# Values of the last two chunks one slot earlier, first keys in four banks, tokens' places one slot later

## The reference

```python
x = x + cross(layernorm(x), ctx)      # 16 heads of 32, stablemax, projections with biases
x = x + self_attention(layernorm(x))  # 8 query heads, one key/value head of 64, causal
x = x + ffn(layernorm(x))             # mean of 2 shared experts + top 2 of 8, hidden 2048
...
shared = (gelu(xf @ sW1 + sb1) @ sW2 + sb2).mean(over the 2 shared)
gates = xf @ rW + rb
topk_vals, topk_idx = top_k(gates, 2)
moe = sum over the chosen e of softmax(topk_vals) * (gelu(xf @ W1[e] + b1[e]) @ W2[e] + b2[e])
return shared + moe
```

## Time and profile before

| | |
|---|---|
| median of 3 runs | 1439.92 us (1439.58 to 1440.78) |
| the profiled execution | 1441.54 us |
| its span, first to last instruction | 1439.8 us |
| TensorE busy | 1390.5 us, 97% |
| VectorE, ScalarE, GpSimd busy | 63%, 56%, 29% |
| TensorE in the chain that ended last | 87% |
| mean granted TensorE clock | 0.987 |

### The profile page before, as it was taken

How to read it: one execution, slowest core, us unless ns; L and a number is a source line. 1 busy time by engine, 2 the same in 40 slices (tenths; PEclk the granted TensorE clock), 3 DMA queues, 4 the chain that set the end, 5 groups by cost and what they waited for, 6 DMA issues and landing times.

```text
span 1439.8 us, 23358 instructions
## 1 busy us (share of the span) xinstructions
PE 1390.5 (97%) x9164; PEld 1252.5 (87%) x9164; DVE 913.5 (63%) x1542; ACT 809.9 (56%) x1453; POOL 414.8 (29%) x219
## 2 busy tenths in 40 slices
PE   6999999999999999999999999879999999999998
PEld 4799999989889889889999989768788999999987
DVE  6456766766776775776675676475566554655665
ACT  3566666655756755756765656454553444545443
POOL 2144353443444434434434434220003000001000
PEclk9999999999999999999999999989999999999999
DMA  5121111011111111011101101084445649999991
GB/s 196 45 92 30 31 34 30 30 63 59 30 70 30 30 63 51 24 60 41 30 30 63 45 30 63 10 347 176 147 154 157 216 162 366 337 354 340 351 397 58
DMA packets 34710, 174.40 MB, mean 121 GB/s; under 512 B 6138, under 2 KB 8346, under 8 KB 18212
## 3 DMA queue, kind: packets, MB, share of 16 engines
q1 hardware_dynamic: 32852, 168.10, 32.6%
q0 software_dynamic: 1744, 4.76, 1.1%
HBM read 166.78 MB, written 6.06 MB: 120 GB/s over the span
## 4 chain that ended last, share of the span: by engine, by line
PE 87%; DVE 6%; ACT 4%; issue 1%; DMA 1%; POOL 0%; PEldq 0%; DVEq 0%; SPq 0%; PEld 0%; POOLq 0%; ACTq 0%
PE bank L680 18%; PE bank L668 17%; PE bank L990 10%; PE bank L700 10%; PE bank L1007 8%; PE po L713 6%; PE bank L852 6%; PE po L869 6%; PE bank L769 1%; PE bank L733 1%; PE bank L725 1%; PE bank L814 1%; DVE tt L1266 1%; ACT tt L1145 1%; DVE sa L1274 1%
## 5 line engine op out<-in xcount | busy, mean ns | idle before, releaser
L552 POOL TENSOR_TENSOR xn<-xn,tt 128x1024 f32<-128x1024 f32 x96 | 237.5, 2474 | 467.4 <-DVE sa L1279 467.4
L1374 DVE TENSOR_TENSOR wsl<-ring,wsh 128x2048 fp32r<-128x2048 f32 x72 | 165.0, 2291 | 118.0 <-ACT wsh L1084 118.0
L668 PE MATMUL bank<-cxh,wkh 128*128 128x256 f32 (+1 forms) x768 | 220.5, 287 | 5.6 <-DVE va L1254 3.2
L668 PE MATMUL bank<-cxl,wkh 128*128 128x256 f32 (+1 forms) x768 | 220.3, 287 | 0.0
L668 PE MATMUL bank<-cxh,wkl 128*128 128x256 f32 (+1 forms) x768 | 220.1, 287 | 0.0
L1247 DVE SCALAR_TENSOR_TENSOR kl<-bank,bkt,kh 128x256 fp32r<-128x256 f32 (+1 forms) x192 | 94.4, 493 | 193.7 <-ACT kh L1042 193.5
L680 PE MATMUL bank<-wvh,cxh 128*128 128x512 f32 (+1 forms) x416 | 165.1, 397 | 2.5 <-DVE kl L1247 2.5
L1140 ACT ACTIVATE tt<-bank 128x512 f32<-128x512 f32 (+1 forms) x208 | 124.1, 599 | 77.0 <-PE bank L700 71.9
L1084 ACT CAST wsh<-ring 128x2048 fp32r<-128x2048 f32 x72 | 137.3, 1907 | 53.2 <-PE po L869 29.6
L680 PE MATMUL bank<-wvl,cxh 128*128 128x512 f32 (+1 forms) x416 | 163.7, 394 | 0.0
L680 PE MATMUL bank<-wvh,cxl 128*128 128x512 f32 (+1 forms) x416 | 163.3, 392 | 0.0
(11 more groups left out here) (237 smaller groups left out, 2954.9 us busy)
## 6 DMA issues: line engine op xcount, KB each, us to landing
ring<-in_w SPq DMA_DIRECT2D x112, 1024.0 KB, 7.0
ctxt<-in_ctx SPq DMA_DIRECT2D x40, 512.0 KB, 3.6
ctxt<-in_ctx SPq DMA_DIRECT2D x8, 642.0 KB, 4.1
wqt<-in_wo SPq DMA_DIRECT2D x4, 1024.0 KB, 5.8
wqt<-in_aq SPq DMA_DIRECT2D x4, 1024.0 KB, 6.4
wqt<-in_ap_ SPq DMA_DIRECT2D x4, 1024.0 KB, 6.4
yrows<-K SPq DMA_DIRECT2D x1, 2048.0 KB, 9.2
tt<-in_wk SPq DMA_DIRECT2D x1, 1024.0 KB, 5.1
```

Of the source, the lines that this page charges most:

```text
L552: e.tensor_tensor(dacc[0:kn, y, :], dacc[0:kn, y, :], tt[0:kn, w, :], ALU.add).then_inc(s["da_pool"], 1)
L668: m = e.matmul(dst[:, 0:n], (wkh, wkl)[a][:, c, g * P:(g + 1) * P], (cxh, cxl)[b][:, u, c, 0:n], start=(c == 0 and x_ == 0), stop=(c == 3 ...
L1374: e.tensor_tensor(wsl[m % 3][:], ring[slot(unit_split(m))][:], wsh[m % 3][:].bitcast(F32), ALU.subtract).then_inc(s["wl_dve"], 1)
```

## The change

Three things. `values_in` gives slot + 2 for every slot up to 101, so chunks 102 and 103 are multiplied in slots 100 and 101. At the start wk is loaded in two halves with part 0 of the context between them, its parts are made in the order of landing, and the keys of part 0 are summed in four banks at once, all groups for each pair of operands (`first_keys`); the warm-up uses `ones`, filled by VectorE, and has 44 matmuls; the values of chunks 0 and 1 move behind the queries on TensorE, ScalarE and VectorE; the turned rows move ahead of the parts of wv; the casts of the patterns and the store of the blank table move back. And `positions` with all that hangs on it moves from `ROUTE` + 1 to `ROUTE` + 2, slot 121 (`PLACE`).

```diff
 ROUTE = NCH + 15
...
 def values_in(slot):
 
-    if slot < NCH - 4:
-        return slot + 2
-    return {NCH - 3: NCH - 2, NCH - 2: NCH - 1}.get(slot)
+    return slot + 2 if slot + 2 < NCH else None
 
...
 
             return 16 * (n // NR + 1)
 
+        def key_bank(i, g):
+            return pj[use["k", i, g] % 2] if i else bank[(0, 1, 4, 5)[g]]
...
                 e.dma_start(ctxt[:, 0:4 * n], ctxs[i % NPT][i // NPT]).then_inc(s["ctx_in"], 16)
 
-            e.dma_start(wkt, wk).then_inc(s["wk_in"], 16)
+            e.dma_start(wkt[:, 0:2, :], wk[:, 0:2, :]).then_inc(s["wk_in"], 16)
             load_ctx(0)
+            e.dma_start(wkt[:, 2:4, :], wk[:, 2:4, :]).then_inc(s["wk2_in"], 16)
             e.dma_start(bkt[:], bk).then_inc(s["bk_in"], 16)
             e.dma_start(xres[:], x).then_inc(s["x_in"], 16)
...
 
-            e.wait_ge(s["zero_dve"], 2)
-            e.dma_start(table.rearrange("(p k) c -> p (k c)", p=P),
...
                 if n == 3:
+                    e.wait_ge(s["zero_dve"], 2)
+                    e.dma_start(table.rearrange("(p k) c -> p (k c)", p=P),
+                                blank[:, :, :].rearrange("p k c -> p (k c)")).then_inc(s["zero_in"], 16)
                     e.wait_ge(s["k2_pool"], 1)
                     e.dma_start(yrows[0:8 * P, :].rearrange("(p a) (b c) -> p (a b) c", p=P, b=2),
...
                             pattern=[[-1, 64]], channel_multiplier=1).then_inc(s["mask_pool"], 1)
             e.wait_ge(s["mask_pool"], 3)
-            e.memset(ones[:], 1.0).then_inc(s["iota_pool"], 1)
+            e.memset(tri[:], 1.0).then_inc(s["iota_pool"], 1)
             e.wait_ge(s["iota_pool"], 1)
...
-            e.wait_ge(s["iota_pool"], 7)
+            e.wait_ge(s["iota_pool"], 6)
             e.memset(qbh[:].bitcast(F32), 0.0).then_inc(s["qz_pool"], 1)
...
                 return pj[u % 2]
+
+            def first_keys():
+
+                n = width(0)
+                for h in range(2):
+                    for x_, (a, b) in enumerate(((0, 0), (1, 0), (0, 1))):
+                        if (h, x_) == (0, 0):
+                            e.wait_ge(s["wkh_act"], 1)
+                            e.wait_ge(s["ch_act"], 1)
+                        elif x_ == 0:
+                            e.wait_ge(s["wkh_act"], 2)
+                        elif x_ == 1:
+                            e.wait_ge(s["wkl_dve"], h + 1)
+                        elif h == 0:
+                            e.wait_ge(s["cl_dve"], 1)
+                        for g in range(4):
+                            for c in (2 * h, 2 * h + 1):
+                                m = e.matmul(key_bank(0, g)[:, 0:n], (wkh, wkl)[a][:, c, g * P:(g + 1) * P],
+                                             (cxh, cxl)[b][:, 0, c, 0:n], start=(x_ == 0 and c == 0),
+                                             stop=(x_ == 2 and c == 3))
+                            if (h, x_) == (1, 2):
...
                     e.wait_ge(s["ch_act"], i + 1)
-                    if i:
-                        e.wait_ge(s["cl_pool"], i)
-                    else:
-                        e.wait_ge(s["wkl_dve"], 2)
-                        e.wait_ge(s["cl_dve"], 1)
+                    e.wait_ge(s["cl_pool"], i)
...
                 m.then_inc(s["pr_pe"], 1)
 
-            e.wait_ge(s["idb_dve"], 1)
-            warm(30, bank[7])
-            for g in range(4):
-                keys(0, g)
-            for n in range(2):
-                values(n)
+            e.wait_ge(s["ones_dve"], 1)
+            warm(44, bank[7])
+            first_keys()
+            e.wait_ge(s["const_pool"], 2)
             for t in range(4):
-                turn(t, bank[2 + t])
+                turn(t, bank[(2, 3, 6, 7)[t]])
             e.wait_ge(s["wq_in"], 16)
...
                 for c in range(4):
                     m = e.matmul(dst[:], wqt[:, c, g * P:(g + 1) * P], xT[:, c, :], start=(c == 0), stop=(c == 3))
                 m.then_inc(s["q_pe"], 1)
+            for n in range(2):
+                values(n)
...
                     shared_up(n - NCH)
-                if n == ROUTE + 1:
+                if n == PLACE:
                     positions()
-                if n == ROUTE + 3:
+                if n == PLACE + 2:
                     turn_weights()
-                if n == ROUTE + 11:
+                if n == PLACE + 10:
                     turn_fetched(0)
                 if n > NCH:
                     shared_down(n - NCH - 1)
-                if n == ROUTE + 5:
+                if n == PLACE + 4:
                     output_biases()
...
                     e.wait_ge(s["s_pe"], 2 * (first(i - 2) + chunks_of(i - 2)))
-                e.activation(kh[:, u, g, 0:n], pj[use["k", i, g] % 2][:, 0:n], ACT.Identity,
+                e.activation(kh[:, u, g, 0:n], key_bank(i, g)[:, 0:n], ACT.Identity,
                              bias=bkt[:, g:g + 1]).then_inc(s["kh_act"], 1)
...
 
             e.preload_act_table_set("natural_log_exp_and_others")
             e.wait_ge(s["wk_in"], 16)
-            for c in (slice(0, 2), slice(2, 4)):
-                e.copy(wkh[:, c, :], wkt[:, c, :]).then_inc(s["wkh_act"], 1)
+            e.copy(wkh[:, 0:2, :], wkt[:, 0:2, :]).then_inc(s["wkh_act"], 1)
             context_hi(0)
+            e.wait_ge(s["wk2_in"], 16)
+            e.copy(wkh[:, 2:4, :], wkt[:, 2:4, :]).then_inc(s["wkh_act"], 1)
             e.wait_ge(s["eps_dve"], 1)
             for t in range(4):
                 root(0, t)
-            keys_hi(0, 0)
-            keys_hi(0, 1)
+            for g in range(4):
+                keys_hi(0, g)
+            turned(0, bank[2])
+            turned(2, bank[6])
             e.wait_ge(s["wv_in"], 16)
             e.copy(wvh[:], wvt[:]).then_inc(s["wvh_act"], 1)
-            keys_hi(0, 2)
-            keys_hi(0, 3)
-            values_hi(0)
-            values_hi(1)
-            turned(0, bank[2])
-            turned(2, bank[4])
             context_hi(1)
...
                              scale=XSCALE).then_inc(s["q_act"], 1)
             for h in range(4):
                 queries_hi(0, h)
+            values_hi(0)
+            values_hi(1)
 
             for n in range(NSLOT):
...
                     e.activation(pr[:, :, 1], pr[:, :, 0], ACT.Exp).then_inc(s["gap_act"], 1)
-                if n == ROUTE + 3:
+                if n == PLACE + 2:
...
                 e.wait_ge(s["kh_act"], 4 * i + g + 1)
-                e.scalar_tensor_tensor(kl[:, u, g, 0:n], pj[use["k", i, g] % 2][:, 0:n], bkt[:, g:g + 1],
+                e.scalar_tensor_tensor(kl[:, u, g, 0:n], key_bank(i, g)[:, 0:n], bkt[:, g:g + 1],
                                        kh[:, u, g, 0:n].bitcast(F32), ALU.add,
...
                 e.tensor_tensor(xres[:, t, :], pj[use["w", t] % 2][:], xres[:, t, :],
                                 ALU.add).then_inc(s["proj_read"], 1)
...
             e.memset(epsb[:], EPS).then_inc(s["eps_dve"], 1)
-            e.wait_ge(s["iota_pool"], 7)
-            e.tensor_copy(iota8[:], iotai[:, 0:8]).then_inc(s["iota_dve"], 1)
-            e.memset(blank[:], 0.0).then_inc(s["zero_dve"], 1)
-            e.wait_ge(s["zero_dve"], 1)
-            e.tensor_copy(blank[:, :, 2], iotai[:, 248:248 + NBLK]).then_inc(s["zero_dve"], 1)
-            e.tensor_copy(kio[:], iotai[:, P:P + 120].rearrange("p (k e) -> p k e", e=8)).then_inc(s["iota_dve"], 1)
-            e.wait_ge(s["const_pool"], 2)
-            e.tensor_copy(identb[:], ident[:]).then_inc(s["idb_dve"], 1)
+            src, hi, lo = ctx_views(0)
...
             for c in range(2):
                 e.wait_ge(s["wkh_act"], c + 1)
                 e.tensor_tensor(wkl[:, 2 * c:2 * c + 2, :], wkt[:, 2 * c:2 * c + 2, :],
                                 wkh[:, 2 * c:2 * c + 2, :].bitcast(F32), ALU.subtract).then_inc(s["wkl_dve"], 1)
-            src, hi, lo = ctx_views(0)
-            e.wait_ge(s["ch_act"], 1)
-            e.tensor_tensor(lo, src, hi.bitcast(F32), ALU.subtract).then_inc(s["cl_dve"], 1)
+                if c == 0:
+                    e.wait_ge(s["ch_act"], 1)
+                    e.tensor_tensor(lo, src, hi.bitcast(F32), ALU.subtract).then_inc(s["cl_dve"], 1)
             e.wait_ge(s["x_in"], 16)
             for t in range(4):
                 stats_of(0, t)
                 if t:
                     rows(0, t - 1)
             rows(0, 3)
-            keys_lo(0, 0)
-            keys_lo(0, 1)
+            turned(1, bank[3])
+            turned(3, bank[7])
+            for g in range(4):
+                keys_lo(0, g)
             e.wait_ge(s["wvh_act"], 1)
             e.tensor_tensor(wvl[:], wvt[:], wvh[:].bitcast(F32), ALU.subtract).then_inc(s["wvl_dve"], 1)
-            keys_lo(0, 2)
-            keys_lo(0, 3)
-            values_lo(0)
-            values_lo(1)
-            turned(1, bank[3])
-            turned(3, bank[5])
             e.wait_ge(s["small_in"], 176)
             e.tensor_scalar(bqs[:], bqt[:], XSCALE, None, ALU.mult).then_inc(s["bqs_dve"], 1)
```

(45 more changed lines are left out.)

## The result

| | before | after |
|---|---|---|
| median | 1440.08 us | 1416.3 us (1414.38 to 1418.57, six runs) |
| ratio of the times | | 0.9834 [0.982, 0.9848] |
| profiled execution | 1441.54 us | 1418.57 us |
| its span | 1439.8 us | 1416.9 us |
| TensorE busy | 1390.5 us, 97% | 1387.7 us, 98% |

The forecast was 1414.5 us, in a range from 1410 to 1420. The same kernel was timed twice more beside the experiments; over its 16 runs it took 1410.39 to 1418.57 us, median 1414.4.

What follows compares the result with a forecast made beforehand. TensorE's work plus its in-order queue's standstills bound the kernel. Gains 10.4 + 2.7 + 9.2 + 1.3 + 2.6 = 26.2 off 1441.54 gave 1415.3, 1413.7 as median, plus 0.8 for low clock: 1414.5 us, range 1410 to 1420.

Steps and rivals of the forecast that it cites:

- Start: Start of the kernel: first scores at 36.95 instead of 47.32, 10.4 us gained, with the values covering the queries' splitting.
- Clock at the start: Behind the first scores, 47 to 53 us: half-speed loss given back when scores follow values directly, 2.7 us.
- Last chunks: End of the attention, scores of chunks 100 to 103: 18.3 us instead of 27.54, 9.2 us gained.
- the weighted sums: From scores(103) to their weighted sum: 1.3 us less at full clock, or nothing if the clock falls again.
- Places: Count of the tokens' places, one slot later: 3.7 us gained, 1.1 lost to a new wait, net 2.6.
- The term for the low clock behind the count: Stretch 1071 to 1074 us behind the count: low clock there costs 1.4 us, given back by the later slot.
- Rival 3: VectorE later behind block starts, last chunks keep the low clock: 1417.2 us; chance 0.14 together with 4.
- 1: Start: clock falls between keys and queries, 1.7 to 3.0 us lost, 1415.4 to 1416.7; chance 0.22 together with 2.
- 2: Start: GpSimd's fills hold VectorE's subtractions until 8.0, 1.9 us missing, 1416.4 us; chance 0.22 together with 1.
- 4: Last stretch: the weight stream bounds it, what the places gain is given back, 1417 us; chance 0.14 with Rival 3.
- 5: Last chunks: ScalarE keeps values of 102 and 103 ahead of the chain, 9.2 + 1.3 stay, 1425 us; chance 0.05.
- 6: Start: slower than before if x lands later than 35 us, each microsecond of delay costing one; chance 0.01.

Runs made afterwards that it cites:

- e2: The kernel after with `values_in` and the place of the count as before, so the new start alone: 1428.47 us, ratio 0.9918.
- e9: The kernel before with one edit, the values of chunks 0 and 1 behind the queries on TensorE, ScalarE and VectorE: 1435.53 us, ratio 0.9963.
- e5: The kernel after once more, unchanged, measured beside other experiments: 1411.61 us, ratio 0.9806.
- e8: The kernel after with the transfer of x behind that of wv: 1416.73 us, ratio 0.9842.
- e1: The kernel before with only `values_in` changed, values of chunks 102 and 103 one slot earlier: 1429.4 us, ratio 0.9933.
- e6: The kernel after with matmuls whose results nobody reads put into five pauses: 1413.47 us, ratio 0.9801.
- e11: The kernel after with the pause-filling matmuls of e6 and the output biases one to a slot: 1412.01 us, ratio 0.9801.

## Why the prediction was right, point by point

**Start.** Foretold 10.4, measured 9.78. The mechanism is as described, e2 and e9 show it, and two terms were a little off. VectorE and ScalarE after:

```profile
6.67 1.23 DVE L1453 TENSOR_TENSOR wkl<-tt,wkh 128x1024 fp32r<-128x1024 f32 x1 [5.54 <-ACT wkh L1122]
7.99 1.23 DVE L1457 TENSOR_TENSOR cxl<-ctxt,cxh 128x1024 fp32r<-128x1024 f32 x1
9.32 1.23 DVE L1453 TENSOR_TENSOR wkl<-tt,wkh 128x1024 fp32r<-128x1024 f32 x1
10.77 0.69 DVE L1300 BATCH_NORM_STATS2 stats<-xres 128x6 f32<-128x512 f32 x1 [0.23 <-DMA xres<-in_x]
...
15.45 0.46 ACT L1060 ACTIVATE kh<-bank,bkt 128x256 fp32r<-128x256 f32 x1
...
33.80 1.32 DVE L1276 TENSOR_TENSOR qbl<-qc,qbh 32x256 fp32r<-32x256 f32 x3
```

The step that was off is the landing of the operands, a microsecond later than estimated (ScalarE's first cast starts at 5.59, not at 4.6), so VectorE is done with the three subtractions only at 10.55 instead of 9.5; and x is there at 10.77 instead of 9.7. The later of the two, x, sets the statistics back by 1.0. From there to the first key copy it is 15.45 - 10.77 = 4.68 against 4.66 foretold. Key copies and turned rows gave back a quarter of a microsecond (queries at 18.19, foretold 17.4), queries and values another 0.2. The splitting of the queries ends at 33.80 + 1.32 = 35.12, under the values that end at 37.54: the cover named for it was there. Why it pays to have the casts gone from the front shows in the same cast of 8 columns, which took 1.85 us beside GpSimd's fill before and takes 0.16 where no fill runs:

```profile
26.48 0.16 DVE L1475 CAST iota<-xa 128x8 f32<-128x8 int32 x1
```

**Clock at the start.** 2.7 foretold, 2.58 measured; e9 gave the same 2.6 on the kernel before.

**Last chunks.** 9.2 foretold, 9.20 measured, with a pause of 1.64 for one of about 1.8. For the weighted sums 1.3 was foretold, 1.10 measured. In e5, where the clock was low again behind scores(103), this term was nothing (7.53 us against the 7.41 of before), which the prediction allowed for.

**Places.** Net 2.6 foretold, 3.04 measured: 4.28 at the count (from the up step of slot 120 to that of slot 121 it is 9.90 us before and 5.62 after) instead of 3.7, and a wait of 0.88 instead of 1.1. The term for the low clock behind the count, put at 1.4, was the one that was too small: 4.28 less the pause of 2.32 is 1.96. Of the 3.40 left behind the new wait, 0.36 went elsewhere up to slot 127.

**What the sum left out.** 9.78 + 2.58 + 9.20 + 1.10 + 3.04 are 25.7 against the 26.2 of the sum, but the span fell by 22.9. The missing 2.7 is the low clock from 922 to 946 us, 0.75 after against 0.87 before: 24 x (0.87 - 0.75) x 2 = 5.8 us more at half speed, 2.9 us lost. The trace hands it on through the ring: the load of aq is issued 35.45 us behind the last weighted sums (957.47) and 32.83 before (977.47), and TensorE waits for it 1.58 and 1.54 us in both. Rival 3 had a part of this ("the last chunks keep the low clock"), but only back to where the kernel before was; that the same pauses could cost more than before was in no case. Nor was it a lasting cost: in e5 the same stretch had 0.87 and the span fell by 30.0. The forecast fell between the two, and that it came within 2 us of the median is in part luck: it holds 0.8 us for a low clock under the queries that no profile shows, and nothing for the stretches near 922 to 946, 990 and 1080 us and for the load of aq, which move this kernel by up to 7 us.

**The rivals.** 1: in no profile of the new start was the clock low under the queries. It was low under the keys in some (9 to 12.7 us in the profile after), and in e8 from 16 to 19.8 us, under the turned rows just ahead of the queries. 2: refuted. The first subtraction started 0.04 us behind its operand and took 1.23 us beside GpSimd's fill (1.21 with GpSimd idle, in the kernel before at 10.61):

```profile
6.20 1.80 POOL L528 MEMSET qbl<- 128x2048 f32 x1
```

That is the narrow form of the rule in the Trainium skill (SBUF — State Buffer, "Who interferes with whom"), by which a fill, which reads nothing, doesn't hold a `tensor_tensor`; the trace agrees with it and not with the broad form. 3: its first half didn't come: the wait is 0.88, less than the 1.1 of the sum, and the clock from 1070 to 1080 is 1.00; of the second see above. 4: refuted, the stream's stretch takes the same 248.8 us, with TensorE busy throughout and the transfers at 0.86. 5: refuted by e1. 6: not slower, x landed at 10.77 us; e8 shows the price per microsecond that was put on it.

## What to carry to other kernels

Look at each place where the in-order engine stands still, ask which later work needs nothing of what it waits for, and put that there: moved values covered the splitting of the queries and kept the clock up, for 7.1 us without removing an instruction. Cost such a move by the chain that is late next, as here ScalarE's and VectorE's weights chain (1.64 us left of 3.93) and the landing of x. And once changes are worth a few tenths of a per cent, compare the granted clock and the landing of loads by stretches before putting a difference, or its absence, down to an edit.

## What the hardware showed

One kernel on one core spread over 8 us (1410.4 to 1418.6) in 16 runs. In the two profiles compared, most of the difference is the granted clock in half a dozen stretches, each behind a pause or the ten-row matmuls (near 8, 920, 940, 990 and 1080 us), of which one run has some and the next others; 1.4 us are a load of 1 MB that was there 7.10 us behind its issue in one and 8.53 in the other.

The clock fell not only behind pauses: with TensorE counted as busy throughout, it was low behind four matmuls with ten rows each in eleven of twelve profiles. What of those matmuls it answers to stays open.

Taking low clock away didn't bring its full worth. Runs of e6 and e11 have mean clocks of 0.995 to 0.999 and take 1410.2 to 1414.1 us, no less than the kernel after at 0.994 to 0.997. Part of the reason is in the profiles: spreading the biases costs 1.1 us, and the 6.8 us of low clock that e6 has less than e5 between 910 and 1000 us brought 1.09 us, not the 3.4 that a busy TensorE would have lost. Whether the filling matmuls cost something besides isn't settled.
